# A graph layer with residual and layer norm: slots of a tile's own neighbours, two-bank buffers, counts on POOL, and a new order of tasks on every engine

## The reference

```python
mask = (adj > 0.0).astype(x.dtype)
W1a, W1b = (W1[:F], W1[F:])
xj_proj = x @ W1a
diff = x[:, :, None, :] - x[:, None, :, :]
h = jax.nn.relu(xj_proj[:, :, None, :] + diff @ W1b + b1)
hm = jnp.einsum('bjkh,bjk->bjh', h, mask)
deg = jnp.sum(mask, axis=-1)
return hm @ W2 + deg[..., None] * b2
```

## Time and profile before

| | |
|---|---|
| three timed runs, us | 307.08, 307.77, 307.98 (median 307.77) |
| the profiled execution, us | 307.45 |
| its span, first to last instruction, us | 305.4 |
| busy in the span: PE, DVE, ACT, POOL | 91%, 89%, 79%, 33% |
| mean granted TensorE clock | 0.981 of full speed |

### The profile page before, as it was taken

The page is one execution under the profiler, slowest core; times in us unless marked ns, Lnnn a source line. Parts: engine busy times, 40 slices in busy tenths (PEclk is TensorE's granted clock), DMA queues, the critical chain, the costliest instruction groups (busy, mean ns, idle before and its releaser), DMA issues. The chain is left out here.

```text
span 305.4 us, 9138 instructions
## 1 busy us (share of the span) xinstructions
PE 277.5 (91%) x2601; PEld 201.4 (66%) x2601; DVE 272.7 (89%) x987; ACT 240.7 (79%) x722; POOL 99.8 (33%) x166
## 2 busy tenths in 40 slices
PE   0386999999999999999999999999999999999960
PEld 0143665868777777758687777777685877766750
DVE  2787799999999999998999999999999999989751
ACT  2329989888898989888998989898979889876500
POOL 2206232323234343334232343434242423304111
PEclk9999999999999999999999999999999999999975
DMA  7930303030302203030403012030303020100000
GB/s 207 364 106 1 89 2 103 3 105 2 96 28 43 80 19 106 17 105 0 120 0 105 15 44 76 18 102 17 103 10 111 1 55 2 38 1 18 19 17 23
DMA packets 28834, 18.13 MB, mean 59 GB/s; under 512 B 17537, under 2 KB 28033, under 8 KB 28802
## 3 DMA queue, kind: packets, MB, share of 16 engines
q1 hardware_dynamic: 28802, 17.76, 20.0%
HBM read 15.65 MB, written 2.10 MB: 58 GB/s over the span
## 5 line engine op out<-in xcount | busy, mean ns | idle before, releaser
L1026 PE MATMUL ring<-hot,vh 128*128 128x256 bf16 (+3 forms) x448 | 96.0, 267 | 1.0 <-ACT ring L742 1.0
L1026 PE MATMUL ring<-hot,vl 128*128 128x256 bf16 (+3 forms) x448 | 95.5, 266 | 0.0
L742 ACT COPY ring<-um 128x512 f32<-128x512 f32 (+2 forms) x144 | 66.0, 476 | 18.1 <-DVE small L1304 10.8
L1295 DVE SCALAR_TENSOR_TENSOR sm<-ring,sm 128x512 f32<-128x512 f32 (+2 forms) x144 | 73.0, 507 | 5.5 <-PE ring L1026 1.9
L1295 DVE SCALAR_TENSOR_TENSOR st<-ring,st 128x256 f32<-128x256 f32 (+2 forms) x144 | 48.1, 334 | 5.2 <-PE ring L1032 1.9
L1026 PEld LDWEIGHTS ring<-hot,vh 128*128 128x128 f16 x448 | 43.7, 98 | 11.7 <-issue 7.5
L1271 DVE TENSOR_SCALAR hot<-slotT 128x1024 bf16<-128x1024 f16 (+2 forms) x144 | 49.4, 374 | 0.0
L742 ACT COPY ring<-ut 128x512 f32<-128x512 f32 (+7 forms) x128 | 38.5, 340 | 13.3 <-DVE st L1295 11.3
L1026 PEld LDWEIGHTS ring<-hot,vl 128*128 128x128 f16 x448 | 43.9, 98 | 2.4
L1032 PE MATMUL ring<-hot,vh 128*64 128x512 bf16 (+3 forms) x256 | 44.7, 352 | 0.0
L533 POOL TENSOR_TENSOR vl<-vf,vh 128x384 f16<-128x384 f32 x32 | 28.6, 914 | 46.6 <-ACT vh L704 46.6
(11 more groups left out here) (106 smaller groups left out, 552.3 us busy)
## 6 DMA issues: line engine op xcount, KB each, us to landing
adj_sb<-adj SPq DMA_DIRECT2D x16, 512.0 KB, 4.3
x_sb<-x SPq DMA_DIRECT2D x16, 128.0 KB, 2.2
x_all<-x SPq DMA_DIRECT2D x4, 512.0 KB, 8.3
xT_sb<-xT SPq DMA_DIRECT2D x16, 128.0 KB, 4.0
out<-o_sb SPq DMA_DIRECT2D x16, 128.0 KB, 2.0
wts<-weights SPq DMA_DIRECT2D x1, 513.0 KB, 6.0
cst_general<-general SPq DMA_DIRECT2D x1, 256.0 KB, 6.2
cst_half<-half SPq DMA_DIRECT2D x1, 113.5 KB, 3.4
```

What stands on the lines that cost most here:

```text
L742: eng.copy(view(segment, ring[unit % BANKS]), u).then_inc(seeded, 1)
L1026: last = eng.matmul(b[:, g * n:g * n + n], part[side][:, g * NT + k, 0:P], selection(g * NT + k), start=(s == 0 and not seeds), stop=(s == ...
L1295: eng.scalar_tensor_tensor(out=to, in0=v, scalar=0.0, in1=to, op0=ALU.max, op1=ALU.add).then_inc(added[tile], 1)
```

## The change

What is changed, beside the diff below:

- **Slots.** The first two slots (`OWN`) hold neighbours in the node's own tile of 128, so each needs one tile's product of 128 columns where the others need both tiles of the graph. The rest has new caps, and six small slots of 6 ranks stand in for seven of 10.
- **Units.** Main and tail of a slot share a unit of two banks (6 groups in place of 4 and 2), and there are 7 units with 2 buffers, in place of 11 with 3. One seed copy and one add cover all six groups (`view`). PE's part is still two tasks, main and tail, which may stand apart.
- **Counts.** DVE makes the mask of a pair in one instruction and the counts in a second (`masks`, `count_masks`); POOL works out degrees, ranks' keys, the excess and the overflow (`count_rest`, `corrections`), in 3 and 12 small instructions. `copy_degrees`, `look_over`, `count_over` and the product with `neg_given` go. `excesses` becomes `excess_main` and `excess_tail`, and one `start_sums` stands for three instructions.
- **x.** It is sorted in fp32 by four products (`perm` is now fp32; `perm16` reads its upper halves), without the split, so `high_x`, `middle_x`, `rest_x` and `low_x` go.
- **Scaling.** It is done on ACT when u and v are copied from PSUM, no longer in the weights; the start has fewer steps, and x and xT of the first pair are loaded behind the first quarter of x.
- **Order.** `number_slots` has twelve products of 128 columns for six of 256. The new `body` runs, for pair p with n the next and o the one before:
  - PE: excess_main p, keys n, gather o2 tail, o3 main, hidden_v p, o3 tail, o4 main, o4 tail, turn_perm p, turn_masks n (graph 0), o5 tail, o5 main, turn_masks n (graph 1), o6 main, number_slots n (0), o6 tail, sort_x n, excess_tail n, p0 tail, p0 main, number_slots n (1), p1 main, project o, p1 tail, hidden_u_main n, unsort_y o, hidden_u_tail n, p2 main.
  - ACT, over the same stretch: ranks n, seed o4, high_v p (0), full_v p (0 and 1), seed o5, high_v p (1), seed o6, copy_maskT n (two), seed p0, seed p1, copy_permT p, copy_slots n (0), copy_xs n, copy_slots n (1), copy_y o, seed p2, deviation, copy_u_main n, copy_u_tail n, seed p3.
  - DVE: start_sums p, add o2, a selection, permutation n, add o3, a selection, add o4, a selection, count_masks, add o5, three selections, clamp_small o, add o6, a selection, reduce_small and add_small o, the small selection, moment, masks, add p0, select_own n (two), add p1, inverse_deviation, a selection, add_residual o, statistics o.
  - POOL: centre, count_rest, neg_keys, degree_bias, scale, residual, corrections, low_v (two).
  - `run` ends after two steps of running out, in place of three.

```diff
-SMALL, NSMALL = 10, 7
-CAPS = [128, 128, 128, 116, 96, 68, 48, 28, 28] + [SMALL] * NSMALL
+OWN = 2
+SMALL, NSMALL = 6, 6
+CAPS = [128, 118, 96, 70, 48, 28, 18, 10] + [SMALL] * NSMALL
 BIG_SLOTS = len(CAPS) - NSMALL
...
+UNITS = [("own", 0), ("own", 1), ("rest", [0]), ("rest", [1]), ("rest", [2]), ("rest", [3, 4]),
+         ("rest", list(range(5, len(CAPS))))]
+NU = len(UNITS)
...
+BUFFERS = 2
...
+        def buffer(pair, unit):
+            w = width(unit)
+            return ring[(pair.side + unit) % BUFFERS][:, 512 - NT * w:512 + TILES * w]
...
+            def count_rest(pair):
+                tiles = counts[pair.side][:, :, :]
+                eng.wait_ge(counted, pair.n + 1)
...
+                eng.tensor_tensor(deg[pair.side][:, :].rearrange("p (g t) -> p g t", g=2), tiles[:, :, 0::NT + 1],
+                                  tiles[:, :, 1:1 + NT], ALU.add).then_inc(deg_ready, 1)
+                own = own_rest[pair.side][:, :].rearrange("p (g t) -> p g t", g=2)
...
+                    eng.tensor_scalar(own, tiles[:, :, 0::NT + 1], -float(OWN), 0.0, ALU.add,
+                                      ALU.max).then_inc(own_rest_ready, 1)
+                eng.wait_ge(own_rest_ready, pair.n + 1)
+                eng.tensor_tensor(rest[pair.side][:, :].rearrange("p (g t) -> p g t", g=2), own, tiles[:, :, 1:1 + NT],
+                                  ALU.add).then_inc(rest_ready, 1)
...
+            def corrections(pair):
+                eng.wait_ge(deg_ready, pair.n + 1)
...
+                eng.wait_ge(ranks_ready, pair.n + 1)
...
+                eng.tensor_tensor(room[:, :, :], const("rank_limits").unsqueeze(2).broadcast_to([P, LIMITS, TILES]),
+                                  rank[:, :].unsqueeze(1).broadcast_to([P, LIMITS, TILES]),
+                                  ALU.subtract).then_inc(room_ready, 1)
+                eng.wait_ge(room_ready, pair.n + 1)
...
+                eng.tensor_tensor(idle_pool[:, :], room[:, 0, 0:1], zeros[:, 0:1], ALU.add)
+                eng.tensor_scalar(above[:, :, :], room[:, :, :], 1.0, 0.0, ALU.min, ALU.max).then_inc(above_ready, 1)
+                eng.wait_ge(above_ready, pair.n + 1)
+                for step, half in enumerate((LIMITS // 2, LIMITS // 4, LIMITS // 8)):
+                    eng.tensor_tensor(above[:, 0:half, :], above[:, 0:half, :], above[:, half:2 * half, :],
+                                      ALU.add).then_inc(folded, 1)
+                    eng.wait_ge(folded, 3 * pair.n + step + 1)
...
+                eng.tensor_tensor(given[:, :], above[:, 0, :], above[:, 1, :], ALU.add).then_inc(given_ready, 1)
+                eng.wait_ge(given_ready, pair.n + 1)
+                eng.tensor_tensor(excess16[pair.side][:, :], deg[pair.side][:, :], given[:, :],
+                                  ALU.subtract).then_inc(excess16_ready, 1)
...
+                eng.tensor_tensor(beyond[:, :], rest[pair.side][:, :], given[:, :], ALU.subtract).then_inc(beyond_ready, 1)
+                eng.wait_ge(beyond_ready, pair.n + 1)
...
+                eng.tensor_tensor(idle_pool[:, :], beyond[:, 0:1], zeros[:, 0:1], ALU.add)
+                eng.tensor_scalar(over[:, :], beyond[:, :], float(OWN), 0.0, ALU.add, ALU.max).then_inc(over_ready, 1)
+                eng.wait_ge(over_ready, pair.n + 1)
+                eng.wait_ge(all_over_ready, pair.n + 1)
+                eng.tensor_tensor(all_over[:, :], all_over[:, :], over[:, :], ALU.add).then_inc(all_over_ready, 1)
...
+                if unit >= BUFFERS:
+                    released(pair, unit - BUFFERS)
...
-                for segment in segments:
-                    groups, _, _, _, slots, cap = segment
-                    u = first_ranks((um if tile == "main" else ut)[pair.side], segment)
-                    u = u.unsqueeze(1 if groups == 1 else 2)
-                    u = u.broadcast_to([P, slots, cap] if groups == 1 else [P, groups, slots, cap])
-                    eng.copy(view(segment, ring[unit % BANKS]), u).then_inc(seeded, 1)
+                    eng.wait_ge(banks_set, 2 * BUFFERS)
+                for segment, (_, slots, cap) in enumerate(SEGMENTS[unit]):
+                    u = u_sb[pair.side][:, :, 0:cap]
+                    if slots > 1:
+                        u = u.unsqueeze(2).broadcast_to([P, GROUPS, slots, cap])
+                    eng.copy(view(pair, unit, segment), u).then_inc(seeded, 1)
...
             def sort_x(pair):
-                eng.wait_ge(xl_ready, pair.n + 1)
+                eng.wait_ge(x_loaded[pair.side], 16 * (pair.half + 1))
                 eng.wait_ge(perm_ready, pair.n + 1)
                 eng.wait_ge(maskT_copied, 2 * pair.n + 2)
-                parts = (xh, xm, xl)
                 for t in range(NT):
-                    for s, part in enumerate(parts):
-                        for g in range(2):
-                            last = eng.matmul(bx2[g * F:g * F + F, t * P:t * P + P], part[:, g * NT + t, :],
-                                              perm[pair.side][:, g * NT + t, :], start=(s == 0),
-                                              stop=(s == len(parts) - 1), skip_group_check=True)
+                    for g in range(2):
+                        eng.matmul(bx2[g * F:g * F + F, t * P:t * P + P], x_sb[pair.side][:, g * NT + t, :],
+                                   perm[pair.side][:, g * NT + t, :], start=True, stop=True, skip_group_check=True)
...
-            def gather(pair, unit):
-                tile, index, _ = UNITS[unit]
+            def gather(pair, unit, part):
                 if unit == 0:
                     eng.wait_ge(vl_ready, 2 * (pair.n + 1))
-                eng.wait_ge(hot_ready, NHOT * pair.n + min(last_slot(unit), NHOT))
+                eng.wait_ge(hot_ready, NHOT * pair.n + selections_of(unit))
                 eng.wait_ge(seeded, NSEED * pair.n + SEEDS_BEFORE[unit + 1])
-                b = ring[unit % BANKS]
-                region, at = region_of(index) if tile == "main" else (index, 0)
-                n = NT * WIDTH[index] if tile == "main" else REGION_COLS[index]
+                own = UNITS[unit][0] == "own"
+                side, b = pair.side, buffer(pair, unit)
+                n = P if own else NT * width(unit)
                 def selection(c):
-                    c0 = REGION_START[region] + c * REGION_COLS[region] + at
-                    return hot[pair.side][:, c0:c0 + n]
-                gather_into(pair.side, b, tile, selection, n).then_inc(gathered, 1)
+                    c0 = HOT_START[unit] + c * n
+                    return hot[side][:, c0:c0 + n]
+                if part == "main":
+                    b = b[:, NT * width(unit):]
+                    for g in range(2):
+                        for s in range(TILES):
+                            k, v = g * NT + s // 2, (vh, vl)[s % 2]
+                            at = k * P if own else g * n
+                            last = eng.matmul(b[:, at:at + n], v[side][:, k, 0:P], selection(k), start=False,
+                                              stop=(s % 2 == 1 if own else s == TILES - 1), skip_group_check=True)
+                else:
+                    for s in range(TILES):
+                        for g in range(2):
+                            k, v = g * NT + s // 2, (vh, vl)[s % 2]
+                            at = s // 2 * P if own else 0
+                            last = eng.matmul(b[g * HT:g * HT + HT, at:at + n], v[side][:, k, P:H], selection(k),
+                                              start=False, stop=(s % 2 == 1 if own else s == TILES - 1),
+                                              skip_group_check=True)
+                last.then_inc(gathered[part], 1)
...
+            def masks(pair):
+                eng.wait_ge(adj_loaded[pair.side], 16 * (pair.half + 1))
+                if pair.follows(2):
+                    eng.wait_ge(maskT_ready, 2 * (pair.n - 1))
+                eng.tensor_scalar(mask[pair.side][:, :, :], adj_sb[pair.side][:, :, :], 0.0, None,
+                                  ALU.is_gt).then_inc(masked, 1)
+            def count_masks(pair):
+                eng.wait_ge(masked, pair.n + 1)
+                if pair.follows(2):
+                    eng.wait_ge(rest_ready, pair.n - 1)
+                    eng.wait_ge(deg_ready, pair.n - 1)
+                eng.tensor_reduce(counts[pair.side][:, :, :].rearrange("p g c -> p (g c)"),
+                                  mask[pair.side][:, :, :].rearrange("p c (k n) -> p (c k) n", k=NT), AX.X,
+                                  ALU.add).then_inc(counted, 1)
             def permutation(pair):
...
+            def add(pair, unit, segment=0):
+                if segment == 0:
+                    eng.wait_ge(gathered["main"], NU * pair.n + unit + 1)
+                    eng.wait_ge(gathered["tail"], NU * pair.n + unit + 1)
...
+                    eng.wait_ge(added, ADDS * pair.n + done)
```

(64 more changed lines are left out.)

1049 lines of the change are left out of this document (454 added, 595 removed).

## The result

The changed kernel takes 309.51 us, median of 13 runs (307.55 to 314.45); the kernel before, timed beside it, 307.08 (305.42 to 308.01, 13 runs). The ratio is 1.0074, 95% interval 1.0045 to 1.0104: 0.7% slower, where 298 us and 3% faster were forecast. The profiled execution took 308.52 for a span of 306.7.

A forecast was written before the change was run, and what follows sets the result against it. PE and DVE were taken as full. PE's 15.35 us plus 0.7 of stalls gave a 16.05 us period; 29.5 + 15 x 16.05 + 25.8 = 296.1 of span, adjusted to 298 us, range 283 to 311.

The forecast's parts named there:

- What bounds the kernel now: Mid-trace, PE was busy 18.00 and DVE 17.60 of 18 us; work must leave both to shorten the period.
- PE after the change: PE's work per pair falls from 16.65 to 15.35 us, mainly from main gathers (-1.10) and tails (-0.57).
- DVE: DVE's work per pair falls by 1.0 to 2.0 us from 16.65; 15.0 taken, under PE's 15.35.
- ACT: ACT's work per pair falls to about 13 us, with four tasks gone and 17 seed copies become 11.
- DVE beside POOL: POOL instructions can hold up DVE's selections: 0.4 us per meeting, 0 to 0.8 a pair, inside DVE's slack.
- Where the new order waits: PE stalls 0.5 us before unit 5's tail and 0.3 before next unit 1's main part; 0.7 a pair taken.
- The walk: Tasks laid out by hand from excess_main at 0, with 0.2 us per hand-over between engines; stalls sum to 0.8 us.
- the ring alone does not bind; only its place in the order does: One buffer's seven units need 22 of 32 us in two periods; the opposing rival, 311 us, had chance 0.12.
- The narrow matmuls: Forecast: 55 ns per 128-column matmul on PE. Rival, chance 0.08: half as long again, likely 308 us.
- POOL's chain: Rival, chance 0.10: low_v waits behind 12 POOL links; beyond 0.40 us each, every 0.1 costs 1.2 us a pair.
- The start: Time before the first pair's first gather: 29.5 us (28 to 32), against 30.7 before.
- The end: From the last pair's first gather on: 25.8 us, with seven units at 11 us and clamp and reduce 0.8 shorter.

The follow-up runs named there:

- e6: Changed kernel with scales() ahead of pair 2's masks and pair 0's low_v ahead of the last four instructions of pair 1's corrections: 307.37 us, no ratio given.
- e2: Changed kernel with unit 6's tail ahead of number_slots on PE, and its clamp and adds ahead of three selections on DVE: 303.13 us, ratio 0.9870.
- e12: Changed kernel with turn_masks(new, 0) issued four times in every body: 312.04 us in a single run, period 16.79 us.
- e8: Changed kernel with four independent 1-element POOL additions ahead of the given counts in each pair: 308.78 us, ratio 1.0055 to the kernel before.
- e9: Changed kernel with turn_perm's transposes issued eight times and sort_x's matmuls three times in the first body alone: 306.94 us, ratio 0.9985 to the kernel before.
- e5: Changed kernel with several gathers, adds and seeds around units 3, 5, 6 and 0 reordered on PE, DVE and ACT: 303.43 us, ratio 0.9885.

## Why the prediction was wrong, step by step

- **What bounds the kernel now** was right: two full engines, and work that leaves both.
- **PE after the change**, 15.35 us (the terms written there add up to 15.37), was right: the period less its three waits, 16.52 - 0.38 - 0.58 - 0.18, is 15.38. Two terms were off and cancel. sort_x took 0.43 (0.66 forecast), its fp32 halves side by side. The seven tails take 3.10 (before, four in 3.32), the main parts 4.97 (5.95): -1.2 in place of -1.37 with the changes of shape.
- **DVE** 15.0: 15.77 of 18 us is 14.5 a period. An add over two banks with 768 elements took 0.95 us, what 1.04 ns an element and 154 fixed make. **ACT** 13: 13.1. **DVE beside POOL**: in the period from 171.37 on, no selection is drawn out beside POOL's 12 small instructions; at the start of e6 four selections beside low_v took 1.98 us, where the changed kernel's same four took 0.57.
- **Where the new order waits: this is the step that failed.** The term was 0.7 us a pair, and the waits are 1.14. The first was forecast at 0.5 and is 0.38, at the place named. The second was forecast at 0.3 and is 0.58. The walk has the clamp and the adds of unit 6 over at 9.6 us; the trace has them over at 10.23 (180.98, counted from excess_main at 170.75), and there the clamp waits for unit 6's tail, which stands behind number_slots on PE. e2 moved the tail ahead of number_slots and gave back 0.34 us a pair. The walk prints no time for this tail, so which of its terms was short isn't known. The third, 0.18 ahead of unit 0's tail, was in no term: "Elsewhere the producer is early by 0.2 us or more" failed at unit 0's seed. To take 0.7 for the walk's own 0.8, since the second wait was hardly larger than an error, went the wrong way. "the ring alone does not bind; only its place in the order does" held: 16.52 became 16.18 with the same two buffers. The waits make 0.44 of the 0.47 by which the period missed 16.05.
- **The narrow matmuls** cost no more: 55 ns each again. The Trainium skill (TensorE: Matmul & The Clock Gate, "Back-to-back issue gap") gives about 81 ns; the traces of this kernel don't agree, with 16 in 0.88 us in e12. **POOL's chain** was given 0.25 to 0.35 for each of 12 links and takes 0.28, and it hides in the loop (e8).
- **The start** failed too: 31.8 against 29.5. scales() waited behind the masks of pair 2, whose adj came late by DMA, and low_v stood behind pair 1's corrections on POOL, of which the price was in the text but only for the loop. e6 moved both at once: 29.3. They were not run apart, but the traces give each its share: ACT's first copy of u starts 1.16 us earlier (21.55 for 22.71), and low_v starts 2.3 us behind the beginning of corrections where it was 3.9. The clock was in no step of the sum: 1.7 us in the profile, 2.6 by e9's medians, in the first interval.
- **The end**: 27.3 against 25.8. "the last pair's seven units, 11 us as before" failed: the last pair's seven units take 12.8 from first to last matmul (279.37 to 292.22; before 10.7, 278.85 to 289.53), with waits for the ring, shown below, and one of 0.58 for a selection, which no other work fills in the drain. (That the lack of other work is the cause was not tried.) What follows the last gather shrank by 1.4 (15.9 to 14.5), more than the 0.8 forecast. PE's timeline of the drain:

```profile
287.96 0.24 PE L1057 MATMUL ring<-hot,vh 128*128 128x192 bf16 x1 [0.51 <-ACT ring L774]
...
289.55 0.29 PE L1064 MATMUL ring<-hot,vh 128*64 128x236 bf16 x2 [0.31 <-ACT ring L774]
...
291.24 0.24 PE L1057 MATMUL ring<-hot,vh 128*128 128x184 bf16 x1 [0.18 <-ACT ring L774]
```

Span: 31.8 + 247.5 + 27.3 = 306.7 against 29.5 + 240.8 + 25.8 = 296.1; of the 10.6 us the periods are 6.7, the start 2.3, the end 1.5. That the periods' part is 15 times the 0.47 missed, less a little, is partly chance: from the first pair's first gather to the second's it is 15.7 us, some 1.7 of them the clock's, and six of the other fourteen starts of the sums lie 16.6 apart and not 16.52.

What stays open: whether the loop can be brought from 16.2 towards PE's 15.4. In e5 A's wait turned into waits for seeds 6 and 0 and into four more changes of array shape; whether an order exists that avoids both was not found.

## What to carry to other kernels

When work leaves every engine and the period stays, look for a closed loop: cut the period at each wait of the fullest engine and add up the pieces; an edit of order is worth only what it takes from a piece, less what it adds to another. A filler of known length in the hole tells at once whether the engine or the loop is the limit, and where it overflows, how large the hole is. Walk a new order through with every small group in it, and ask of each wait which of its sources ends last: six matmuls of 0.055 us each ahead of a tail that a clamp waits for, four small instructions ahead of `low_v`, one wait for a DMA ahead of a scale and the clock that followed were the way from 309 to 299 us. An instruction that stands right ahead of a late one need not be what it waits for.

## What was not expected of the hardware

- TensorE's granted clock fell to 0.50 for over 4 us after a stretch with 2.1 to 2.4 us of matmuls in 4, in some executions and not in others; matmuls of 128 columns then lie 0.11 us apart (31.83 to 31.94, two halves side by side) instead of 0.06. With 44 more matmuls by the page's count in that stretch it was 1.00.
- In the middle of the trace the loop repeats to 0.01 us, with or without 0.55 us of extra matmuls in its holes.
- Between matmuls of the full array and those of half of it some 0.10 to 0.13 us pass, and a wait hides them. The Trainium skill (TensorEngine Tiling (Array Packing), "Key Properties") says that a change of tiling mode drains the engine; the 0.13 us of e12 fit that.
